# Two steps of attention share one phase of value matmuls from step 12 on

## What is computed

```python
scores = jnp.einsum('bqhd,bkhd->bhqk', q, k) * scale
weights = jax.nn.softmax(scores, axis=-1)
out = jnp.einsum('bhqk,bkhd->bqhd', weights, v)
...
x = x + _layernorm(attn(_layernorm(x)))      # q, k, v, o projections inside
x = x + _layernorm(ffn(_layernorm(x)))       # sigmoid(xr@Wr) * (square(relu(xk@Wk))@Wv), xr/xk mix x with x_prev
```

## Time and profile before

| | before |
|---|---|
| median of three runs | 1271.68 us (1270.45 to 1273.1) |
| the profiled execution | 1271.37 us |
| its span in the profile | 1269.6 us |
| TensorE busy | 1250.9 us, 99% |
| ScalarE busy | 1065.5 us, 84% |
| VectorE busy | 781.7 us, 62% |
| GpSimd busy | 269.1 us, 21% |
| granted TensorE clock | full speed throughout |

### The profile page before, as it was taken

How to read it: one execution, slowest core, us unless ns; L and a number is a source line. 1 busy time by engine, 2 the same in 40 slices (tenths; PEclk the granted TensorE clock), 3 DMA queues, 4 the chain that set the end, 5 groups by cost and what they waited for, 6 DMA issues and landing times.

```text
span 1269.6 us, 25462 instructions
## 1 busy us (share of the span) xinstructions
PE 1250.9 (99%) x10604; PEld 601.9 (47%) x10604; DVE 781.7 (62%) x1738; ACT 1065.5 (84%) x1155; POOL 269.1 (21%) x351
## 2 busy tenths in 40 slices
PE   8999999999999999999999999999999999999997
PEld 5544454444444445454544444444444444534345
DVE  7644746658465773847557584666747466364647
ACT  4788888888888888888888888888888888898872
POOL 2000212222211322222121221222221122222121
PEclk9999999999999999999999999999999999999999
DMA  4455564317712194124733166321751129400000
GB/s 154 128 133 170 103 128 79 92 51 132 119 51 84 52 181 85 52 66 105 147 68 112 43 112 130 76 84 51 149 118 45 42 68 177 91 1 18 18 16 19
DMA packets 61796, 112.69 MB, mean 89 GB/s; under 512 B 6512, under 2 KB 31344, under 8 KB 61616
## 3 DMA queue, kind: packets, MB, share of 16 engines
q1 hardware_dynamic: 61360, 109.60, 38.3%
q10 hardware_dynamic: 288, 1.05, 0.3%
HBM read 68.42 MB, written 41.94 MB: 87 GB/s over the span
## 4 chain that ended last, share of the span: by engine, by line
PE 94%; DVE 2%; ACT 2%; DMA 1%; issue 0%; POOL 0%; SPq 0%; DVEq 0%
PE O L480 39%; PE S L470 27%; PE M L425 24%; PE M L373 3%; PE M L401 2%; ACT PT L538 2%; DMA xA<-x_dram 1%; DVE sth L728 0%; DVE A L736 0%; DVE QS L690 0%; ACT QS L566 0%; DVE A L988 0%; DVE xB L858 0%; POOL rsh L1089 0%; DVE st L676 0%
## 5 line engine op out<-in xcount | busy, mean ns | idle before, releaser
L538 ACT ACTIVATE PT<-S 128x1024 f32<-128x1024 f32 x1024 | 1003.3, 1026 | 158.4 <-PE S L470 157.7
L480 PE MATMUL O<-PT,V 128*17 128x512 f32 x4096 | 538.9, 598 | 0.1
L470 PE MATMUL S<-QS,KS 50*128 50x512 f32 x2048 | 465.5, 450 | 3.7 <-ACT PT L538 3.7
L470 PEld LDWEIGHTS S<-QS,KS 50*128 50x128 f32 x2048 | 211.1, 184 | 453.1 <-ACT PT L538 376.4
L480 PEld LDWEIGHTS O<-PT,V 128*17 128x17 f32 x4096 | 67.9, 95 | 140.3 <-issue 137.6
L1087 POOL TENSOR_SCALAR veh<-mvh 128x2 f32<-128x2 f32 x96 | 22.3, 232 | 489.2 <-DVE mvh L731 487.5
L988 DVE SCALAR_TENSOR_TENSOR A<-Z,M 128x512 f32<-128x512 f32 x30 | 20.4, 682 | 159.4 <-PE M L425 159.4
L425 PE MATMUL M<-xnT,WH 64*128 64x512 f32 x496 | 108.0, 393 | 0.0
L425 PE MATMUL M<-WH,xnT 64*128 64x256 f32 x480 | 79.6, 278 | 0.0
L425 PE MATMUL M<-WH,C 64*128 64x256 f32 x480 | 78.6, 278 | 0.8 <-issue 0.8
L425 PE MATMUL M<-WH,cT 64*128 64x256 f32 x480 | 78.7, 278 | 0.0
(11 more groups left out here) (152 smaller groups left out, 1648.5 us busy)
## 6 DMA issues: line engine op xcount, KB each, us to landing
scr<-p SPq DMA_DIRECT2D x124, 256.0 KB
QS<-scr SPq DMA_DIRECT2D x56, 256.0 KB, 6.5
KS<-scr SPq DMA_DIRECT2D x56, 256.0 KB, 10.5
QS<-scr SPq DMA_DIRECT2D x70, 128.0 KB, 5.7
KS<-scr SPq DMA_DIRECT2D x68, 128.0 KB, 8.0
xA<-x_dram SPq DMA_DIRECT2D x16, 512.0 KB, 7.1
xB<-x_dram SPq DMA_DIRECT2D x16, 512.0 KB, 7.3
out_dram<-xB SPq DMA_DIRECT2D x15, 512.0 KB, 3.1
```

What stands on the lines that cost most here:

```text
L470: ins = e.matmul(PS[pair][:, a, :], KS[qd][rows, pair, kt * 128:kt * 128 + 128], QS[qd][rows, pair, hf * 512:hf * 512 + 512], start=True, ...
L480: ins = e.matmul(PO[32 * j:32 * j + 17, :], V[b % 2][:, kt, 4 * qd + j, :], PT[i % 2][:, j, :], start=(kt == 0), stop=(kt == 7))
L538: e.activation(PT[i % 2][:, 2 * pair:2 * pair + 2, :], PS[pair][:, :, :], ACT.Exp, scale=SCALE) \
```

## The change

From step 12 (`PAIRED`) on TensorE works in periods of two steps: scores that are still missing for the second step (`LATE`, three heads), a part of the halves of both steps, turns, more halves, five heads' scores ahead (`AHEAD`: head 1 of step i + 3, then the four heads of step i + 2, where the period holds steps i and i + 1) between the halves, then the values of both steps. The scores wait for a bank each and no longer for a pair (`HEAD_BANKS`: head 1 of odd steps has a fifth bank), so of the seven banks beside O five belong to heads and two are left to the pieces; the first turn of a pair uses head 1's bank. ScalarE has five exponentials a period in place of four, two of them of one head (128x512). The exponentials have three buffers PT. `outputs` stands in the period after the quad's end, behind the exponential of heads 2 and 3, and the quad's stages begin one step later. VectorE copies y out of its bank first (into A) and T00 and T10 (into On) first, and does the rest from SBUF. In FIRST and LAST some pieces begin one step earlier or later so that they fall on even steps. Two small tensors of the range branch share other memory, and three steps of unit 0 place one row half differently.

```diff
+PAIRED = 12
+LATE = ((1, 0), (1, 2), (1, 3))
+AHEAD = ((1, 1), (0, 0), (0, 1), (0, 2), (0, 3))
+HEAD_BANKS = ((0, 1, 2, 3), (0, 4, 2, 3))
...
-FIRST = {2: "V2", 3: "K01", 4: "V3", 5: "Q10", 6: "K10", 7: "K11", 8: "Q01", 9: "Q11", 11: "T0", 15: "Q00", 17: "K00",
-         19: "T1", 23: "Q01", 25: "K01"}
+FIRST = {2: "V2", 3: "K01", 4: "V3", 5: "Q10", 6: "K10", 7: "K11", 8: "Q01", 9: "Q11", 12: "T0", 14: "Q00", 16: "K00",
+         18: "T1", 22: "Q01", 24: "K01"}
 NEXT_TO_LAST = {2: "V3", 4: "y0", 6: "y1", 14: "z", 20: "k0", 22: "k1", 24: "r0", 26: "r1", 28: "v0", 30: "v1"}
-LAST = {4: "y0", 6: "y1", 13: "z", 17: "k0", 19: "k1", 21: "r0", 23: "r1", 25: "v0", 27: "v1"}
+LAST = {4: "y0", 6: "y1", 12: "z", 16: "k0", 18: "k1", 20: "r0", 22: "r1", 24: "v0", 26: "v1"}
...
-STAGES = {"y": 3, "v": 2}
+STAGES = {"y": 3, "v": 2, "T": 2}
...
+    if word in ("T01", "T11"):
+        return 1
...
-        rest = [(("quad", i // 8), 0)] if i % 8 == 7 else []
+        done = i if i < PAIRED else i - 1
+        rest = [(("quad", done // 8), 0)] if done % 8 == 7 else []
...
+    fifth, free = free[0], free[1:]
+    at = {0: ("exp", PAIRED, 0), 1: ("exp", PAIRED, 1), 2: ("exp", PAIRED, 2), 3: ("exp", PAIRED, 3), 4: fifth[1]}
+    number = [0, 1, 2, 3, fifth[0]]
+
+    def take_for(i, j):
+        k = HEAD_BANKS[i % 2][j]
+        of[i, j], freed[i, j], at[k] = number[k], at[k], ("exp", i, j)
+
+    for i in range(PAIRED, STEPS, 2):
+        for user in late_heads(i):
+            take_for(*user)
         if TURNS[i]:
-            take(TURNS[i])
-            leave(TURNS[i], 0)
-        for piece, stage in RESTS[i]:
-            leave(piece, stage)
+            of[TURNS[i]], freed[TURNS[i]], at[1] = number[1], at[1], ("bank", TURNS[i])
+            take(TURNS[i + 1], free)
+            free.append(left(TURNS[i + 1]))
+        elif HALVES[i][0]:
+            take(HALVES[i][0][0], free)
+        for user in ahead_heads(i):
+            take_for(*user)
+        if not TURNS[i]:
+            free += [left(piece) for piece, _ in ENDS[i + 1]]
...
-        PT = [sb(f"PT{i}", [128, 4, 512]) for i in range(2)]
+        PT = [sb(f"PT{i}", [128, 4, 512]) for i in range(3)]
...
-        PS = [ctx.enter_context(nc.psum_tensor(f"S{i}", [128, 2, 512], F32)) for i in range(2)]
+        PB = ctx.enter_context(nc.psum_tensor("M", [128, 7, 512], F32))
         PO = ctx.enter_context(nc.psum_tensor("O", [128, 512], F32))
-        PM = [ctx.enter_context(nc.psum_tensor(f"M{i}", [128, 512], F32)) for i in range(3)]
+        PS = [PB[:, 2 * i:2 * i + 2, :] for i in range(2)]
+        PM = [PB[:, k, :] for k in range(7)]
...
+            def gather(i):
+
                 for row, half_ in enumerate(HALVES[i]):
                     if half_:
                         piece, part = half_
                         every = list(moving_of(*piece)(rows_of(row)))
                         mine = every if part == 2 else every[part * len(every) // 2:(part + 1) * len(every) // 2]
-                        left[row] = [(piece, part != 1 and k == 0, part and k + 1 == len(mine), len(every), *one)
-                                     for k, one in enumerate(mine)]
+                        left[row] += [(piece, part != 1 and k == 0, part and k + 1 == len(mine), len(every), *one)
+                                      for k, one in enumerate(mine)]
+
+            def halves(enough=99.0):
+
                 while left[0] or left[1]:
                     row = 1 if not left[0] or left[1] and took[1] < took[0] else 0
+                    if took[row] > enough:
+                        break
...
+            def period(i):
+
+                late, ahead = late_heads(i), ahead_heads(i)
+                took[:] = 0.0, 0.0
+                for n in range(2):
+                    gather(i + n)
+                for one in late[:-2]:
+                    score(*one)
+                halves(.1)
+                for one in late[-2:]:
+                    score(*one)
+                for n in range(2):
+                    if TURNS[i + n]:
+                        turn(TURNS[i + n])
+                halves(.55)
+                if ahead:
+                    if heads[i + 2][3] == 0:
+                        maxima(*heads[i + 2][:3], i + 2)
+                    score(*ahead[0])
+                    halves(1.25)
+                    for one in ahead[1:3]:
+                        score(*one)
+                halves()
+                for one in ahead[3:5]:
+                    score(*one)
+                values(i)
+                values(i + 1)
...
-            def exponentials(i, pair):
-                if i == STEPS:
+            def exponentials(i, *numbers):
+
+                if i >= STEPS:
                     return
-                p.wait_ge(("scores", i, pair))
-                if i >= 2:
-                    p.wait_ge(("values", i - 2))
-                e.activation(PT[i % 2][:, 2 * pair:2 * pair + 2, :], PS[pair][:, :, :], ACT.Exp, scale=SCALE) \
-                    .then_inc(*up(act_wrote, ("exp", i, pair)))
+                j, k, at = numbers[0], numbers[-1], bank[i, numbers[0]]
+                p.wait_ge(("scores", i, j), ("scores", i, k))
+                if i >= 3:
+                    p.wait_ge(("values", i - 3))
+                e.activation(PT[i % 3][:, j:k + 1, :], PB[:, at:at + len(numbers), :], ACT.Exp, scale=SCALE) \
+                    .then_inc(*up(act_wrote, *[("exp", i, n) for n in numbers]))
...
+                for word, n in filter(None, TURNS[8 * g:8 * g + 8]):
+                    if word in ("T00", "T10"):
+                        p.wait_ge(("xnT", n, 0, int(word[1])))
...
+                exponentials(i + 1, 0)
+                if i == PAIRED:
+                    exponentials(i + 1, 1)
+                exponentials(i + 1, 2, 3)
+                if i % 8 == 0:
+                    outputs(i // 8 - 1)
+                exponentials(i + 2, 0, 1)
+                for (word, n), stage in ENDS[i + 1]:
                     if word[0] == "r":
                         sigmoids(n, int(word[1]))
-                exponentials(i + 1, 1)
-                if i % 8 == 7 and i < STEPS - 1:
-                    outputs(i // 8)
+                exponentials(i + 2, 2, 3)
+                exponentials(i + 3, 1)
...
+                elif stage == 0:
+                    p.wait_ge(("piece", piece), ("On_turned", (turned_at(piece) - 1) // 8 - 1))
+                    e.tensor_copy(On[:, :], m[:, :]).then_inc(*note(("bank", piece)))
+                else:
+                    p.wait_ge(("bank", piece), ("piece", ((("K10", "Q11"), ("V1", "V3"))[b > 1][g], b - 1)))
+                    e.tensor_copy(xnT[0][:, c, cols], On[:, :]).then_inc(*note(("hi", piece)))
+                    lower(xnT[1][:, c, cols], On[:, :], xnT[0][:, c, cols].bitcast(F32), ("hi", piece), ("xnT", b, c, g))
...
+                copy, here = A[:, 512 * g:512 * g + 512], ("piece", piece)
+                if stage == 0 and u < UNITS - 1:
+                    p.wait_ge(("piece", piece), *a_free(u))
+                    e.tensor_copy(copy, m[:, :]).then_inc(*note(("bank", piece)))
+                if u < UNITS - 1:
+                    m, here = copy, ("bank", piece)
...
-                        normed("y", u, g, t, At[:, 2 * g + t, :], m[:, t * 256:t * 256 + 256], *a_free(u))
-                    up(dve_wrote, ("bank", piece), by=0)
+                        normed("y", u, g, t, At[:, 2 * g + t, :], At[:, 2 * g + t, :])
```

## The result

The changed kernel takes 1299.75 us (median of 4 runs, 1298.18 to 1300.98) against 1271.66 us before: 1.022 of the time, 95% interval 1.0202 to 1.0237. The prediction was 1267 us with a range of 1226 to 1300 and "faster" as the likeliest; the median is just inside the range, at its far end, and on the other side of no change. The time is that of rival 2, the slower side, but that is luck in part: its make-up was another.

The account below looks back on a forecast made before the run. TensorE's own order of work was taken as the bound: 1271.4 - 72 (filled periods) - 2 (turns) + 3.6 (empty periods) + 6 (output copy) = 1207, plus 60 of bank waits = 1267 us; range 1226 to 1300.

Parts of the forecast that it names:

- rival 2: Two-bank waits cost more than the seams: 80 us of waits plus 13 for half-empty rows, 1300 us; chance 0.16.
- The seam saving: Values of two steps in one phase: 0.34 us saved a period, 72 us over 211 filled periods.
- rival 3: A second set of values has its seam too: 1302 us; chance 0.12 together with rival 4.
- rival 4: TensorE's issue limits periods with 256-column pieces, about 120 saving nothing: 1290 us; chance 0.12 together with rival 3.
- The bank waits: TensorE waits for VectorE to empty one of the pieces' two banks: together 60 us lost.
- the empty periods: Ten periods without halves or turns: a loop through ScalarE sets 4.30 us against 3.94 before, 3.6 us lost.
- Rival 1: The banks come free in time, 15 to 25 us of waits remain: 1227 us; chance 0.22.
- The row phase: Scores and halves in a filled period: 2.50 us, with values a period of 4.37 instead of 4.71.
- The turn periods: 29 periods holding transpositions: 4.47 us instead of 4.54 for two steps, 2 us saved.
- Steps 8 to 12: VectorE's queue ahead of a bank's release: wait 1.2 us in odd units (V0), 1.1 in even.
- steps 1 to 4: VectorE's queue before Q10's bank is free at 10.3 us; y0 waits 1.0 in odd units, 0.45 in even without LN1.
- The late copy of O: ScalarE's output copy behind heads 2 and 3 delays the values by 0.1 us at 62 quads: 6 us lost.

Follow-up runs that it names:

- zyheld: zheld with the second stage of y1 also held to step 11 and odd units' LN1 statistics moved from step 2 to 4; 1232.75 us, 0.9696 of before.
- filled_whole: Changed kernel with 14 or 9 extra 128-row matmuls (even or odd units) in step 20's period, ahead of the bank wait; 1287.75 us, 1.0132 of before.
- zheld: Changed kernel with the third and fourth later stages of z held from steps 18 and 19 to 20 and 22; 1249.85 us, 0.983 of before.
- filled: Changed kernel with one 50-row score repeated 14 or 9 times (even or odd units) in step 20's period, ahead of the bank wait; 1292.68 us, 1.0188 of before.

## Why the prediction was wrong, point by point

**The seam saving was right.** 4.71 for two steps, 4.37 forecast, 4.38 measured where both pieces have 512-column matmuls. Two sets of values stand side by side without a seam: 1.84. The Trainium skill (TensorEngine Tiling, Key Properties) ties the drain to a change of tiling mode; the trace agrees with its 1.84 us, and rival 3 is out. Periods with 256-column pieces alone take 4.38 to 4.40 where no quad begins, so rival 4, a limit of issue near 4.7, is out as well.

**The bank waits were right, in place and size.** Forecast 3.4 at k0 of even units, measured 3.46; 2.15 at k0 of odd units, measured 2.0 to 2.5; 1.2 at V0, measured 1.13; 1.0 at y0, measured 1.27; 1.1 around T10 and T11, measured 0.71; 0.45 at y0 of even units, measured 0.48. The sum of TensorE's standing still rose by 63 us (18.7 to 82.2) where 60 was forecast; 3 of the 63 are waits for exponentials (3.7 to 7.1), which the forecast held elsewhere, in the empty periods. Adding up VectorE's queue from the start-to-start times of the earlier trace rows was enough for this. Rival 1, banks that come free in time, fell with it. zyheld shows what it described, 1232.75 against its 1227, once the queue's order is right.

**The step that failed is the price of the waits in the sum.** It priced a wait at its length, and two terms were missing from the sum and from the rivals.

One is the clock. At ten of the thirteen waits at k0 the granted clock fell to the lower level, which cost 16 us in all by zheld and 16 by filled_whole, and some 2.5 us at 84 to 92 besides. The page before showed full speed throughout, and the longest standstill in it was 1.5 us; I took that row as given for the kernel after, though the same text forecast waits of 3.4 us in it.

The other is the restart, about 0.27 us behind each wait for a bank. The changed kernel has 37 of them behind the first 100 us, so 10 us.

The clock alone doesn't decide the sign: with the waits at k0 filled and no lower clock behind the first 100 us, filled_whole is still at 1287.75, of which some 3 us are the filling in unit 0.

**A second term was mis-sized.** The row phase was taken at its ideal sum for every kind of piece. Filled periods without a wait and without a quad's beginning take 4.39 on the mean in place of 4.37, 4 us in all. The turn periods take 4.60 (615.81 to 620.41) in place of 4.47, since five scores with two turns ahead of them take 1.08: 4 us. The turn periods before were taken too dear as well: 0.66 + 0.59 + 0.98 to 1.0 is 2.24 a step and 4.48 for two, not 4.54, so they had 2 us less to give. That makes 10. I had named the half-empty row as part of rival 2, at 0.1 in half the periods; it is less.

Two chains of VectorE's queue were added up slightly wrong too. Steps 8 to 12 give 1.1, not 1.2; steps 1 to 4 give 10.1 and a wait of 0.8, not 10.3 and 1.0. Together that is 2 us.

The sum with all of it, an estimate from the rows above: 1207 + 60 of waits + 10 of restarts + 18.5 of clock + 10 for the mis-sized periods, less 3 for the copy of O that came out at half its price, is 1302.5. The profiled execution took 1300.98.

**ScalarE** was right: three wide and two narrow exponentials fit in with 0.55 us idle a period. The late copy of O cost 0.04 to 0.05 a quad (4.43 where a quad begins), forecast 0.1.

**The chances** were the other failing. A forecast 5 us from no change, the difference of two terms of 64 and 60 us, the second a wait whose side effects were unknown, deserved more on the slower side than 0.36.

## What to carry to other kernels

Before taking a buffer away from a producer that never waits, add up the consumer's in-order queue in front of each release, and reorder that queue in the same change; here the order alone was worth 67 us in the kernel with two banks, 50 of them by two stages of z, and these two were worth nothing with three. Price a wait of TensorE at its length plus a restart (0.27 us here) plus what the granted clock loses behind it, even where the kernel before shows full speed. Keep phases of different array shapes long: a way into the values and out of it cost 0.34 us among long phases and 0.46 on the mean where a phase of three scores was squeezed between two.

## What the hardware showed that I had not expected

- Behind a standstill of 3.46 us TensorE ran at the lower level for most of 4 us (0.57 of full speed over 709 to 713). The clock fell at all six waits of 3.5 us at k0 of even units, three times while TensorE still stood, and at four of the seven of 2.0 to 2.5 us in odd units. The length alone doesn't tell which: the one of 2.51 us had no drop, one of 2.02 us had. Once those waits were gone (zheld) it fell nowhere between the first 100 and the last 10 us.
- A wait costs more than the idle time in the profile: 0.26 to 0.29 us more, by three waits of 2.2 to 2.5 us with the clock at full speed.
- Busy time by the profile doesn't keep the level: in filled TensorE worked through the wait on 50 of 128 rows and the level still fell in four places; on all 128 rows, with other operands, it fell in none. The Trainium skill (TensorE: Matmul & The Clock Gate, Part 1) says that the clock is throttled by default and released by activity, and the trace agrees: in the changed kernel every stretch at the lower level behind the first 100 us begins in or behind a standstill. Why 50 rows at work were not enough in some places is left open.
- Three scores and one matmul of the halves squeezed between two sets of values took 0.88 us, two matmuls of 512 columns on each row half, where the sum of their columns is 0.43.
